# The last layer of a four-layer kernel scheduled anew: context part one batch ahead, product taken through the output weight first

## The chip, the cores and the metric

The kernel runs on one core of a Trainium2 chip. The metric is the device time of one execution, in microseconds; three runs of the kernel before gave 4614.44, 4619.2 and 4638.48 us, median 4619.2.

## The reference, cut to what matters

Four layers run one after the other on x (8 batches of 256 x 512, float32). The change touches only the last, a non-local block that takes the residual stream x and the context x_2, both per batch 256 channels by 512 positions:

```python
def _L3_xattn_ref(x, x_2, ...):
    B, C, CI, N = (16, 256, 128, 512); EPS = 1e-05
    g_x     = conv1x1(g_w, g_b, x_2).transpose(0, 2, 1)      # [b, 512, 128]
    theta_x = conv1x1(theta_w, theta_b, x).transpose(0, 2, 1)
    phi_x   = conv1x1(phi_w, phi_b, x_2)                     # [b, 128, 512]
    W = einsum('bnc,bcm->bnm', theta_x, phi_x) / 512
    y = einsum('bnm,bmc->bnc', W, g_x).transpose(0, 2, 1)
    wy = conv1x1(w_w, w_b, y)
    wy = bn_gamma * (wy - bn_mean) * rsqrt(bn_var + EPS) + bn_beta
    return wy + x
```

No softmax stands between the products, so they may be taken in any order. Both kernels first form M = phi g / 512 (128 x 128, from the context alone). The kernel before then has Y = M' theta and O = w_w Y.

## The kernel before, in words

The kernel is built by `layer0` to `layer3`, each with its own buffers, its own semaphores and one program per engine; a barrier ends each layer. Layer 2 ends with two stores of x3T to DRAM (L1783). Layer 3 works on 8 batches (B = 8), one after another, in rolled loops (`Fori`) on all engines. P = 128, E = 512, L = 256, CI = 128, LC = 2 (channel chunks), EC = 4 (position chunks). Everything in layer 3 is float32.

SyncE (SP) first adds 128 to each of its 21 semaphores (`start_ahead`, L2614, helper at L47), so that waits on a loop counter's value are never on zero; then it loads six constants (L2616) and, per batch, XT (the layer's input, transposed, L2623) and C (the context, L2624), once TensorE has finished with the batch before: there is one buffer of each.

TensorE per batch: eight 128x128 transposes of XT into banks 0 and 1 (L2643); eight matmuls for phi and g of the four position chunks, C the stationary operand, moving width 256, into banks 2 and 3 (L2649); two for theta, width 512 (L2654); four for M, width 128 (L2658); one for Y, width 512 (L2662); two for O, width 512, again into banks 2 and 3 (L2665). The profile counts each float32 matmul as two MATMUL instructions, except the transposes, which are one each.

ScalarE copies the transposed input out to X (L2678), theta with its bias to TH (L2680), and Y (L2682). VectorE adds the phi and g bias (L2698, writes PG), scales M (L2701), then per output chunk applies scale and shift of the batch norm (L2705), drains (L2706, which frees the banks for the next L2649), adds X (L2707) and drains (L2708, which frees X for the next L2678). GpSimd (POOL) stores the whole 256 x 512 output of a batch in one DMA from its queue (L2631), and lets O be written again when the store has landed.

The order around the change is thus set by the program order of each engine and by the semaphores; nothing is planned at run time.

Of the kernel before, what the change touches and what calls it, by code (L numbers as in the profile page):

```python
# [2577 lines left out]
def layer3(nc, x3T, ctx, theta_w, pg_w, pg_b, w_w, vec3, ident_in, out):  # L2578
    with ExitStack() as stack:
        def sb(name, shape, dt=F32):  # L2580
            return stack.enter_context(nc.sbuf_tensor("d_" + name, shape, dt))
# [24 lines left out]
        names = "consts_in memset_done bn_sqrt bn_in x_in in_used x_ps x_ready pg_ps pg_ready m_ps m_ready th_ps th_ready y_ps y_ready o_ps o_read out_ready out_free passed".split()  # L2606
        (consts_in, memset_done, bn_sqrt, bn_in, x_in, in_used, x_ps, x_ready, pg_ps, pg_ready, m_ps, m_ready, th_ps, th_ready,
         y_ps, y_ready, o_ps, o_read, out_ready, out_free, passed) = [sem(n) for n in names]
        out_stored = stack.enter_context(nc.semaphore("d_out_stored"))
        block = stack.enter_context(nc.Block())  # L2610

        @block.sync
        def _(sp):
            start_ahead(sp, sems)  # L2614
            for dst, src in ((WT[:, :, :], theta_w), (WPG[:, :, :], pg_w), (BPG[:, :], pg_b), (WW[:, :], w_w), (VEC[:, :], vec3), (ID[:, :], ident_in)):
                sp.dma_start(dst, src).then_inc(consts_in, 16)  # L2616
            with sp.Fori(0, B) as b:

                sp.wait_ge(x_ps, b + AHEAD)
                sp.sem_inc(passed, 1)  # L2620
                sp.wait_ge(pg_ps, b + AHEAD)
                sp.sem_inc(passed, 1)
                sp.dma_start(XT[:, :, :], x3T[b]).then_inc(x_in, 16)  # L2623
                sp.dma_start(C[:, :, :], ctx[b].rearrange("(k p) t -> p k t", p=P)).then_inc(x_in, 16)  # L2624
        @block.gpsimd
        def _(pool):
            pool.memset(EPS[:, :], LN_EPS).then_inc(memset_done, 1)
            with pool.Fori(0, B) as b:
                pool.wait_ge(out_ready, b + 1 + AHEAD)
                pool.sem_inc(passed, 1)  # L2630
                pool.dma_start(out[b].rearrange("(k p) t -> p k t", p=P), O[:, :, :]).then_inc(out_stored, 16)  # L2631
                pool.wait_ge(out_stored, (b + 1) * 16)
                pool.sem_inc(out_free, 1)

        @block.tensor
        def _(pe):
            pe.wait_ge(consts_in, 96 + AHEAD)
            pe.wait_ge(memset_done, 1 + AHEAD)
            with pe.Fori(0, B) as b:
                pe.wait_ge(x_in, (b + 1) * 32 + AHEAD)  # L2640
                for c in range(LC):
# [17 lines left out]
                mm.then_inc(m_ps, 1)
                pe.wait_ge(m_ready, b + 1 + AHEAD)  # L2660
                pe.wait_ge(th_ready, b + 1 + AHEAD)
                pe.matmul(ps[:, 6, :], M[:, :], TH[:, :], start=True, stop=True).then_inc(y_ps, 1)  # L2662
                pe.wait_ge(y_ready, b + 1 + AHEAD)
# [4 lines left out]
        @block.scalar
        def _(act):
            act.wait_ge(memset_done, 1 + AHEAD)  # L2670
            act.wait_ge(consts_in, 96 + AHEAD)
# [2 lines left out]
            with act.Fori(0, B) as b:
                act.wait_ge(x_ps, b + 1 + AHEAD)

                act.wait_ge(in_used, b + AHEAD)
                act.activation(X[:, :, :], ps[:, 0:2, :], ACT.Copy).then_inc(x_ready, 1)  # L2678
                act.wait_ge(th_ps, b + 1 + AHEAD)
                act.activation(TH[:, :], ps[:, 5, :], ACT.Identity, bias=VEC[:, V3_TB:V3_TB + 1]).then_inc(th_ready, 1)  # L2680
                act.wait_ge(y_ps, b + 1 + AHEAD)
                act.activation(Y[:, :], ps[:, 6, :], ACT.Copy).then_inc(y_ready, 1)  # L2682

        @block.vector
        def _(dve):
            dve.wait_ge(bn_sqrt, 1 + AHEAD)
# [9 lines left out]
            with dve.Fori(0, B) as b:  # L2696
                dve.wait_ge(pg_ps, b + 1 + AHEAD)
                dve.tensor_tensor(PG[:, :, :], ps[:, 2:4, :].rearrange("p a (c t) -> p (a c) t", c=2),  # L2698
                                  BPG[:, :].unsqueeze(1).broadcast_to([P, EC, 2 * CI]), ALU.add).then_inc(pg_ready, 1)
                dve.wait_ge(m_ps, b + 1 + AHEAD)  # L2700
                dve.tensor_scalar(M[:, :], ps[:, 4, 0:CI], 1.0 / E, None, ALU.mult).then_inc(m_ready, 1)  # L2701
                dve.wait_ge(o_ps, b + 1 + AHEAD)
                dve.wait_ge(out_free, b + AHEAD)
                for c in range(LC):
                    dve.tensor_scalar(O[:, c, :], ps[:, 2 + c, :], BN[:, 0, c:c + 1], BN[:, 1, c:c + 1], ALU.mult, ALU.add)  # L2705
                dve.drain().then_inc(o_read, 1)  # L2706
                dve.tensor_tensor(O[:, :, :], O[:, :, :], X[:, :, :], ALU.add).then_inc(out_ready, 1)  # L2707
                dve.drain().then_inc(in_used, 1)  # L2708
# [120 lines left out]
```

## Time and profile before

| quantity | value |
|---|---|
| median of 3 runs | 4619.2 us (4614.44 to 4638.48) |
| the profiled execution | 4615.37 us, span 4613.7 us |
| mean granted TensorE clock | 0.966 of full speed |
| TensorE matmul busy, whole kernel | 4238.2 us (92%) |
| VectorE busy | 2998.3 us (65%) |
| ScalarE busy | 1928.3 us (42%) |
| GpSimd busy | 1659.0 us (36%) |
| last matmul of layer 2 starts | 4487.84 us |
| first work of TensorE in layer 3 | 4505.61 us |
| end of the span | 4613.7 us |

Times are from the start of the span. The span runs from the first to the last instruction. A busy TensorE means that some matmul is in flight: matmuls are pipelined, and the distance between starts is what one costs. The granted clock is the share of full TensorE speed that the chip allowed in a stretch.

### The profile page before, as it was taken

What the parts mean: (1) busy time and instruction counts of PE and PEld (TensorE: products, weight loads), DVE (VectorE), ACT (ScalarE), POOL (GpSimd) and SP (SyncE); (2) the same over time, 40 slices, a digit from 0 to 9 for tenths busy, and PEclk for the clock granted to TensorE, in tenths of its full rate; (3) what the DMA queues carried; (4) which work ended last, traced back from release to release, by engine and by line L of the source; (5) the groups of instructions that cost most, each with busy time, mean ns of one, the idle gap of its engine ahead of it and who ended that gap; (6) DMA issues with size and microseconds to landing.
All of it is one profiled execution on the core that took longest, in us unless ns stands there. A gap on an engine that the chain in (4) does not pass through costs nothing. (4 is left out here: it accounts for less than half of the span.)

```text
span 4613.7 us, 72508 instructions
## 1 busy us (share of the span) xinstructions
PE 4238.2 (92%) x22864; PEld 3208.3 (70%) x22864; DVE 2998.3 (65%) x6494; ACT 1928.3 (42%) x3748; POOL 1659.0 (36%) x1139
## 2 busy tenths in 40 slices
PE   6999999578999997599999999999999999999987
PEld 3444444356777775488787797887887877978864
DVE  5666665178888885375775775766767757757543
ACT  2555555212232321255552454552554534545511
POOL 1222342345555553233334323234333344332330
PEclk8999999789999997799999999999999999999999
DMA  1000000200000000222112312222222122122223
GB/s 38 25 23 25 19 24 10 115 5 10 15 15 15 15 19 10 68 68 74 61 60 71 99 60 69 65 65 81 86 65 70 60 67 90 57 73 61 61 69 115
DMA packets 126449, 242.02 MB, mean 52 GB/s; under 512 B 16884, under 2 KB 38132, under 8 KB 124928
## 3 DMA queue, kind: packets, MB, share of 16 engines
q1 hardware_dynamic: 123904, 230.61, 15.9%
q0 software_dynamic: 2304, 8.39, 0.4%
q8 instruction: 127, 2.08, 0.2%
q14 instruction: 114, 0.93, 0.1%
HBM read 221.91 MB, written 16.78 MB: 52 GB/s over the span
## 5 line engine op out<-in xcount | busy, mean ns | idle before, releaser
L1885 POOL TENSOR_TENSOR c_wl<-c_wr,c_wh 128x512 fp32r<-128x512 f32 (+1 forms) x576 | 823.2, 1441 | 1672.2 <-ACT c_wh L2197 1465.9
L2291 ACT ACTIVATE c_pr<-c_ps,c_nms 128x257 f32<-128x257 f32 x512 | 244.5, 478 | 481.8 <-DVE c_nms L2485 479.3
L583 ACT ACTIVATE a_ex<-a_ps 128x1024 f32<-128x1024 f32 x256 | 261.4, 1024 | 260.4 <-PE a_ps L419 260.3
L1482 DVE TENSOR_TENSOR_SCAN b_sb<-b_wt,b_s,b_ps 128x256 f32<-128x256 f32 x512 | 362.1, 736 | 11.7 <-DVE b_ps L1468 1.4
L683 DVE TENSOR_REDUCE a_nm<-a_ps 128x2 f32<-128x1024 f32 x256 | 311.4, 1221 | 81.0 <-PE a_ps L396 80.8
L1434 POOL TENSOR_TENSOR b_sb<-b_sb,b_rt 128x1024 f32<-128x1024 f32 x128 | 278.2, 2180 | 207.5 <-ACT b_sb L1363 122.3
L1944 PE MATMUL c_ps<-c_hh,c_wh 128*128 128x512 f32 x768 | 318.2, 414 | 33.3 <-POOL c_hl L1891 33.1
L1944 PE MATMUL c_ps<-c_gh,c_wh 128*128 128x512 f32 x768 | 307.9, 401 | 23.5 <-DVE c_gl L2523 17.7
L2197 ACT ACTIVATE c_wh<-c_wr 128x512 fp32r<-128x512 f32 (+1 forms) x464 | 316.3, 688 | 8.6 <-PE c_ps L1946 7.4
L1944 PE MATMUL c_ps<-c_wh,c_cth 128*128 128x256 f32 x1024 | 304.7, 298 | 9.3 <-DVE c_ctl L2438 5.0
L1946 PE MATMUL c_ps<-c_hh,c_wl 128*128 128x512 f32 x768 | 309.9, 403 | 0.0
L1945 PE MATMUL c_ps<-c_hl,c_wh 128*128 128x512 f32 x768 | 309.6, 403 | 0.0
L1946 PE MATMUL c_ps<-c_gh,c_wl 128*128 128x512 f32 x768 | 303.2, 395 | 0.0
L1945 PE MATMUL c_ps<-c_gl,c_wh 128*128 128x512 f32 x768 | 302.9, 394 | 0.0
L1946 PE MATMUL c_ps<-c_wh,c_ctl 128*128 128x256 f32 x1024 | 290.6, 284 | 0.0
L1945 PE MATMUL c_ps<-c_wl,c_cth 128*128 128x256 f32 x1024 | 289.5, 283 | 0.0
L433 PE MATMUL a_ps<-a_ex,a_vf 128*64 128x512 f32 x1024 | 278.9, 623 | 8.9 <-ACT a_ex L583 7.9
L2483 DVE TENSOR_REDUCE c_nm<-c_ps 128x1 f32<-128x257 f32 x512 | 214.9, 420 | 69.1 <-PE c_ps L1946 68.4
L1040 PE MATMUL b_ps<-b_xf,b_w 128*128 128x256 f32 x1024 | 238.2, 386 | 13.0 <-DVEq L1533 9.1
L1040 PEld LDWEIGHTS b_ps<-b_xf,b_w 128*128 128x128 f32 x1024 | 194.0, 193 | 48.2 <-issue 17.9
L2523 DVE TENSOR_TENSOR c_gl<-c_g,c_gh 128x512 fp32r<-128x512 f32 x128 | 95.4, 752 | 201.6 <-ACT c_gh L2278 201.6
L2479 DVE TENSOR_SCALAR c_pr<-c_pr,c_rs 128x257 f32<-128x257 f32 x512 | 184.8, 361 | 40.3 <-issue 0.8
(309 smaller groups left out, 10762.7 us busy)
## 6 DMA issues: line engine op xcount, KB each, us to landing
c_wr<-in_downs SPq DMA_DIRECT2D x192, 256.0 KB, 2.7
c_wr<-in_wv SPq DMA_DIRECT2D x64, 512.0 KB, 3.8
c_wr<-in_wk SPq DMA_DIRECT2D x128, 256.0 KB, 2.9
c_wr<-in_wq SPq DMA_DIRECT2D x128, 256.0 KB, 2.7
c_wr<-in_fc SPq DMA_DIRECT2D x64, 256.0 KB, 2.8
b_w<-in_w SPq DMA_DIRECT2D x8, 1024.0 KB, 14.4
a_x<-in_x SPq DMA_DIRECT2D x8, 512.0 KB, 3.4
a_ctx<-in_ctx SPq DMA_DIRECT2D x8, 512.0 KB, 4.1
```

Of the source, the lines that this page charges most:

```text
L433: mm = pe.matmul(ps[64 * a:64 * a + VCOLS, BO, :], VF[:, k, g * HG + 2 * p + a, :], EX[:, n % 4, a, :], start=(k == 0), stop=(k == EC - 1) ...
L583: act.activation(EX[:, n % 4, :, :], ps[:, BT + 2 * (n % 2):BT + 2 * (n % 2) + 2, :], ACT.Exp).then_inc(ex_ready, 1)
L683: dve.tensor_reduce(NM[:, s, :].rearrange("p (h c) -> p h c", h=HG)[:, 2 * p:2 * p + 2, c:c + 1], ps[:, bank:bank + 2, :], AX.X, ALU.max, ...
L1040: mm = pe.matmul(half(bank, o), W[:, w, k, o * P:(o + 1) * P], src[:, k, :], start=(k == 0), stop=(k == EC - 1), skip_group_check=True)
L1434: pool.tensor_tensor(SB[:, quad % RING, :, 0:L], SB[:, quad % RING, :, 0:L], RT[:, third(b, q // 4), q // 4 % 2, :].unsqueeze(1).broadcast ...
L1482: mm = dve.tensor_tensor_scan(SB[:, quad % RING, r, 1:L + 1], WT[:, third(b, c), c % 2, :], half(spread_bank(pair), r), S0[:, b % 2, c, 4 ...
L1885: pool.tensor_tensor(piece(WL, slot), piece(WR, slot), piece(WH, slot), ALU.subtract).then_inc(piece_cut[slot], 1)
L1944: pe.matmul(out, sh, mh, start=start, stop=False, skip_group_check=True)
L1945: pe.matmul(out, sh, ml, start=False, stop=False, skip_group_check=True)
L1946: return pe.matmul(out, sl, mh, start=False, stop=stop, skip_group_check=True)
L2197: act.activation(piece(WH, slot), piece(WR, slot), ACT.Copy).then_inc(piece_high[slot], 1)
L2291: act.activation(PR[:, i, 0:L + 1], ps[:, BS + 1 - i % 2, 0:L + 1], ACT.Exp, bias=NMS[:, i:i + 1], scale=float(K2) ** -0.5, accum_out=RS[: ...
```

## The change: what it does

The input buffers XT and C, the output buffer O and a new buffer XB have two halves, used by batch parity. All five programs are unrolled in Python (no `Fori`), so no semaphore is moved ahead. TensorE does turn and phi_and_g (the first two steps) of batch b+1 before the last step of batch b. M is formed with its operands swapped, so that one matmul of width 256 can take it through the output weight: N = M' w_w (128 x 256); then O = N' theta, two matmuls of width 512, into banks 6 and 7. Y is gone. ScalarE also writes XB, which is X plus the shift of the batch norm, per chunk. VectorE ends a chunk with one scalar_tensor_tensor (O = scale * psum + XB) and no drain; each chunk is stored on its own from SP's queue. The constants are issued partly from SP, partly from ScalarE, in an order by need. The diff, without the lists of semaphore names and, from the SP program on, without most removed lines (they are printed above):

```diff
-        XT = sb("xt", [P, EC, L])
-        C = sb("c", [P, LC, E])
+        XT = sb("xt", [P, 2, EC, L])
+        C = sb("c", [P, 2, LC, E])
         X = sb("x", [P, LC, E])
+        XB = sb("xb", [P, 2, LC, E])
         PG = sb("pg", [P, EC, 2 * CI])
         M = sb("m", [P, CI])
+        N = sb("n", [P, L])
         TH = sb("th", [P, E])
-        Y = sb("y", [P, E])
-        O = sb("o", [P, LC, E])
+        O = sb("o", [P, 2, LC, E])
...
+        xt_in = [sem(f"xt_in{i}") for i in range(2)]
+        c_in = [sem(f"c_in{i}") for i in range(2)]
+        out_stored = [sem(f"out_stored{i}") for i in range(2)]
+        BXT, BPGS, BMN, BTH, BOUT = 0, 2, 4, 5, 6
...
 
         @block.sync
         def _(sp):
...
+            def load_ctx(b):
+                sp.dma_start(C[:, b % 2], ctx[b].rearrange("(k p) t -> p k t", p=P)).then_inc(c_in[b % 2], 16)
+            def load_x(b):
+                sp.dma_start(XT[:, b % 2], x3T[b]).then_inc(xt_in[b % 2], 16)
+            sp.dma_start(WPG[:, :, :], pg_w).then_inc(pg_in, 16)
+            load_ctx(0)
+            load_x(0)
+            sp.dma_start(WT[:, :, :], theta_w).then_inc(w_in, 16)
+            load_ctx(1)
+            load_x(1)
+            for b in range(B):
+                if b + 2 < B:
+                    sp.wait_ge(pg_ps, b + 1)
+                    load_ctx(b + 2)
+                    sp.wait_ge(x_ps, b + 1)
+                    load_x(b + 2)
+                for c in range(LC):
+                    sp.wait_ge(o_read, b * LC + c + 1)
+                    sp.dma_start(out[b, c * P:(c + 1) * P], O[:, b % 2, c, :]).then_inc(out_stored[b % 2], 16)
+            for i in range(2):
+                sp.wait_ge(out_stored[i], B // 2 * LC * 16)
         @block.gpsimd
         def _(pool):
             pool.memset(EPS[:, :], LN_EPS).then_inc(memset_done, 1)
...
 
         @block.tensor
         def _(pe):
...
+            def turn(b):
+                if b >= 1:
+                    pe.wait_ge(xb_ready, b)
+                if b == 0:
+                    pe.wait_ge(x_const_in, 3 * 16)
+                pe.wait_ge(xt_in[b % 2], (b // 2 + 1) * 16)
                 for c in range(LC):
                     for k in range(EC):
...
+                        mm = pe.transpose(ps[:, BXT + c, k * P:(k + 1) * P], XT[:, b % 2, k, c * P:(c + 1) * P], ID[:, :])
                 mm.then_inc(x_ps, 1)
 
...
+            def phi_and_g(b):
+                if b == 0:
+                    pe.wait_ge(pg_in, 16)
+                pe.wait_ge(c_in[b % 2], (b // 2 + 1) * 16)
                 for m in range(EC):
                     for k in range(LC):
...
+                        mm = pe.matmul(ps[:, BPGS + m // 2, (m % 2) * L:(m % 2 + 1) * L], C[:, b % 2, k, m * P:(m + 1) * P], WPG[:, k, :],
                                        start=(k == 0), stop=(k == LC - 1), skip_group_check=True)
                 mm.then_inc(pg_ps, 1)
...
+            def product(b):
+                pe.wait_ge(pg_ready, b + 1)
+                for m in range(EC):
+                    mm = pe.matmul(ps[:, BMN, 0:CI], PG[:, m, CI:], PG[:, m, 0:CI], start=(m == 0), stop=(m == EC - 1), skip_group_check=True)
+                mm.then_inc(m_ps, 1)
+            def theta(b):
+                if b == 0:
+                    pe.wait_ge(w_in, 2 * 16)
+                pe.wait_ge(x_ready, b + 1)
                 for k in range(LC):
...
+                    mm = pe.matmul(ps[:, BTH, :], WT[:, k, :], X[:, k, :], start=(k == 0), stop=(k == LC - 1))
                 mm.then_inc(th_ps, 1)
...
+            def through_w(b):
+                pe.wait_ge(m_ready, b + 1)
+                pe.matmul(ps[:, BMN, CI:CI + L], M[:, :], WW[:, :], start=True, stop=True, skip_group_check=True).then_inc(n_ps, 1)
+            def result(b):
+                pe.wait_ge(n_ready, b + 1)
+                pe.wait_ge(th_ready, b + 1)
                 for c in range(LC):
...
+                    if b >= 1:
+                        pe.wait_ge(o_read, (b - 1) * LC + c + 1)
+                    pe.matmul(ps[:, BOUT + c, :], N[:, c * P:(c + 1) * P], TH[:, :], start=True, stop=True).then_inc(o_ps, 1)
+            phi_and_g(0)
+            turn(0)
+            product(0)
+            theta(0)
+            through_w(0)
+            for b in range(B):
+                if b + 1 < B:
+                    turn(b + 1)
+                    phi_and_g(b + 1)
+                result(b)
+                if b + 1 < B:
+                    product(b + 1)
+                    theta(b + 1)
+                    through_w(b + 1)
 
         @block.scalar
         def _(act):
...
+            for dst, src in ((BPG[:, :], pg_b), (ID[:, :], ident_in), (VEC[:, :], vec3)):
+                act.dma_start(dst, src).then_inc(x_const_in, 16)
+            act.dma_start(WW[:, :], w_w).then_inc(w_in, 16)
+            act.wait_ge(memset_done, 1)
+            act.wait_ge(x_const_in, 3 * 16)
             act.activation(BN[:, 0, :], VEC[:, V3_VAR:V3_VAR + 2], ACT.Sqrt, bias=EPS[:, 0:1]).then_inc(bn_sqrt, 1)
...
+            for b in range(B):
+                act.wait_ge(x_ps, b + 1)
+                if b >= 1:
+                    act.wait_ge(th_ps, b)
+                act.activation(X[:, :, :], ps[:, BXT:BXT + 2, :], ACT.Copy).then_inc(x_ready, 1)
+                if b == 0:
+                    act.wait_ge(bn_ready, 1)
+                if b >= 2:
+                    act.wait_ge(o_read, (b - 1) * LC)
+                for c in range(LC):
+                    mm = act.activation(XB[:, b % 2, c, :], ps[:, BXT + c, :], ACT.Identity, bias=BN[:, 1, c:c + 1])
+                mm.then_inc(xb_ready, 1)
+                act.wait_ge(th_ps, b + 1)
+                act.activation(TH[:, :], ps[:, BTH, :], ACT.Identity, bias=VEC[:, V3_TB:V3_TB + 1]).then_inc(th_ready, 1)
+                act.wait_ge(n_ps, b + 1)
+                act.activation(N[:, :], ps[:, BMN, CI:CI + L], ACT.Copy).then_inc(n_ready, 1)
 
         @block.vector
         def _(dve):
...
+            def add_bias(b):
+                dve.wait_ge(pg_ps, b + 1)
+                if b == 0:
+                    dve.wait_ge(x_const_in, 3 * 16)
+                dve.tensor_tensor(PG[:, :, :], ps[:, BPGS:BPGS + 2, :].rearrange("p a (c t) -> p (a c) t", c=2),
+                                  BPG[:, :].unsqueeze(1).broadcast_to([P, EC, 2 * CI]), ALU.add).then_inc(pg_ready, 1)
+            def take_product(b):
+                dve.wait_ge(m_ps, b + 1)
+                dve.tensor_scalar(M[:, :], ps[:, BMN, 0:CI], 1.0 / E, None, ALU.mult).then_inc(m_ready, 1)
+            def finish(b):
+                dve.wait_ge(xb_ready, b + 1)
+                if b >= 2:
+                    dve.wait_ge(out_stored[b % 2], b // 2 * LC * 16)
+                for c in range(LC):
+                    dve.wait_ge(o_ps, b * LC + c + 1)
+                    dve.scalar_tensor_tensor(O[:, b % 2, c, :], ps[:, BOUT + c, :], BN[:, 0, c:c + 1], XB[:, b % 2, c, :], ALU.mult, ALU.add).then_inc(o_read, 1)
+            dve.wait_ge(bn_sqrt, 1)
             dve.reciprocal(BN[:, 0, :], BN[:, 0, :])
             dve.tensor_tensor(BN[:, 1, :], VEC[:, V3_WB:V3_WB + 2], VEC[:, V3_MEAN:V3_MEAN + 2], ALU.subtract)
             dve.drain()
@@ -2693,20 +2768,15 @@
             dve.tensor_tensor(BN[:, 1, :], BN[:, 1, :], BN[:, 0, :], ALU.mult)
             dve.drain()
             dve.tensor_tensor(BN[:, 1, :], BN[:, 1, :], VEC[:, V3_BETA:V3_BETA + 2], ALU.add)
...
+            dve.drain().then_inc(bn_ready, 1)
+            add_bias(0)
+            take_product(0)
+            for b in range(B):
+                if b + 1 < B:
+                    add_bias(b + 1)
+                finish(b)
+                if b + 1 < B:
+                    take_product(b + 1)
 
 
 def _l0(I):
```

## Rows read from the trace of the kernel before

**Rows 1.** The chain of waits, 4480 us to the end: shares by line.

```profile
by line: PE d_ps L2649 22.6%; PE d_ps L2665 11.4%; PE d_ps L2654 9.8%; PE d_ps L2662 6.5%; PE d_ps L2658 5.2%; DVE d_o L2705 4.6%; DVEq L2706 4.3%; ACT d_y L2682 3.5%; issue 3.4%; DMA d_c<-in_ctx 3.3%; SPq L2616 1.8%; DVE d_m L2701 1.7%; PE
```

**Rows 2.** Stretches: their us, busy us per engine, granted clock, DMA share, GB/s.

```profile
4440.00:4488.00 48.00, 48.00 (x208) 38.54 (x206) 22.54 (x35) 5.51 (x8) 18.10 (x14) 1.00 0.20 60
4488.00:4505.60 17.60, 0.22 (x1) 0.00 (x0) 1.72 (x7) 1.58 (x2) 0.10 (x1) 0.59 0.50 161
4533.90:4546.10 12.20, 10.31 (x42) 6.67 (x42) 4.27 (x5) 2.31 (x3) 0.73 (x1) 1.00 0.37 129
```

**Rows 3.** Timeline of one batch: start, us, engine, line, operation [idle before].

```profile
4533.91 3.72 PE L2649 MATMUL d_ps<-d_wpg,d_c 128*128 128x256 f32 x16 [0.87 <-DVEq L2706]
4533.95 1.22 DVE L2707 TENSOR_TENSOR d_o<-d_o,d_x 128x1024 f32<-128x1024 f32 x1
4535.26 1.02 ACT L2678 ACTIVATE d_x<-d_ps 128x1024 f32<-128x1024 f32 x1 [5.12 <-DVEq L2708]
4537.47 1.88 PE L2654 MATMUL d_ps<-d_x,d_wt 128*128 128x512 f32 x4
4537.67 1.23 DVE L2698 TENSOR_TENSOR d_pg<-d_ps,d_bpg 128x1024 f32<-128x1024 f32 x1 [2.50 <-PE d_ps L2649]
4538.95 1.10 PEld L2658 LDWEIGHTS d_ps<-d_pg 128*128 128x128 f32 x8 [0.43 <-DVE d_pg L2698]
4539.19 1.05 PE L2658 MATMUL d_ps<-d_pg 128*128 128x128 f32 x8
4539.39 0.69 ACT L2680 ACTIVATE d_th<-d_ps,d_vec 128x512 f32<-128x512 f32 x1 [3.11 <-PE d_ps L2654]
4540.62 1.12 PE L2662 MATMUL d_ps<-d_th,d_m 128*128 128x512 f32 x2 [0.38 <-DVE d_m L2701]
4541.79 0.60 ACT L2682 ACTIVATE d_y<-d_ps 128x512 f32<-128x512 f32 x1 [1.71 <-PE d_ps L2662]
4542.44 1.98 PE L2665 MATMUL d_ps<-d_y,d_ww 128*128 128x512 f32 x4 [0.69 <-ACT d_y L2682]
4544.26 1.04 PE L2643 MATMUL d_ps<-d_id,d_xt 128*128 128x128 f32 x8
4544.55 1.53 DVE L2705 TENSOR_SCALAR d_o<-d_ps,d_bn 128x512 f32<-128x512 f32 x2 [3.98 <-PE d_ps L2665]
4546.16 3.72 PE L2649 MATMUL d_ps<-d_wpg,d_c 128*128 128x256 f32 x16 [0.87 <-DVEq L2706]
```

**Rows 4.** The chain of waits into layer 3: start, us, what.

```profile
4495.59 0.02 SPq L47
...
4497.26 0.33 SPq L2616
...
4500.93 4.64 DMA d_c<-in_ctx
```

**Rows 5.** Stretches as in Rows 2: where the clock rises, and elsewhere.

```profile
4511.00:4512.00 1.00, 1.00 (x4) 0.80 (x4) 0.00 (x0) 0.00 (x0) 0.00 (x0) 0.65 0.00 0
...
1400.00:1500.00 100.00, 98.37 (x538) 77.76 (x537) 86.48 (x130) 29.97 (x63) 60.02 (x29) 1.00 0.02 6
...
4390.00:4400.00 10.00, 5.45 (x11) 3.38 (x12) 6.30 (x8) 2.52 (x4) 5.93 (x4) 0.50 0.15 39
```

**Rows 6.** Timeline of the last batch's end.

```profile
4607.45 1.23 DVE L2707 TENSOR_TENSOR d_o<-d_o,d_x 128x1024 f32<-128x1024 f32 x1
4609.42 0.72 POOL L2631 DMA_DIRECT2D out<-d_o  x1 [11.52 <-DVE d_o L2707]
```

**Rows 7.** Layer 2's operation of the added kind, by line: ns min/median/max.

```profile
L2386 DVE SCALAR_TENSOR_TENSOR c_x<-c_ps,c_vec,c_x x48: 733/750/753, 2184.9 to 4488.3; 128x512 f32<-128x512 f32 x48
```

**Rows 8.** DMA issues by line: KB each, median us from issue to landing.

```profile
d_c<-in_ctx SPq DMA_DIRECT2D x8, 512.0 KB, 4.8
out<-d_o POOLq DMA_DIRECT2D x8, 512.0 KB, 3.1
...
c_wr<-in_downs SPq DMA_DIRECT2D x192, 256.0 KB, 2.7
```

More of the change, by code:

```diff
@@ L2581, in sb @@
             return stack.enter_context(nc.sbuf_tensor("d_" + name, shape, dt))
-        sems = []
         def sem(name):
-            sems.append(stack.enter_context(nc.semaphore("d_" + name)))
-            return sems[-1]
+            return stack.enter_context(nc.semaphore("d_" + name))
         WT = sb("wt", [P, LC, CI])
@@ L2596, in layer3 @@
         BN = sb("bn", [P, 2, 2])
-        XT = sb("xt", [P, EC, L])
-        C = sb("c", [P, LC, E])
+        XT = sb("xt", [P, 2, EC, L])
+        C = sb("c", [P, 2, LC, E])
         X = sb("x", [P, LC, E])
+        XB = sb("xb", [P, 2, LC, E])
         PG = sb("pg", [P, EC, 2 * CI])
         M = sb("m", [P, CI])
+        N = sb("n", [P, L])
         TH = sb("th", [P, E])
-        Y = sb("y", [P, E])
-        O = sb("o", [P, LC, E])
+        O = sb("o", [P, 2, LC, E])
         ps = stack.enter_context(nc.psum_tensor("d_ps", [P, 8, 512], F32))
[L2606 to L2609, printed above, removed]
+        names = "pg_in x_const_in w_in memset_done bn_sqrt bn_ready x_ps x_ready xb_ready pg_ps pg_ready m_ps m_ready th_ps th_ready n_ps n_ready o_ps o_read".split()
+        (pg_in, x_const_in, w_in, memset_done, bn_sqrt, bn_ready, x_ps, x_ready, xb_ready, pg_ps, pg_ready, m_ps, m_ready, th_ps, th_ready,
+         n_ps, n_ready, o_ps, o_read) = [sem(n) for n in names]
+        xt_in = [sem(f"xt_in{i}") for i in range(2)]
+        c_in = [sem(f"c_in{i}") for i in range(2)]
+        out_stored = [sem(f"out_stored{i}") for i in range(2)]
+        BXT, BPGS, BMN, BTH, BOUT = 0, 2, 4, 5, 6
         block = stack.enter_context(nc.Block())
@@ L2613, in _ @@
         def _(sp):
[L2614 to L2624, printed above, removed]
+            def load_ctx(b):
[19 more added lines that the diff above has]
+                sp.wait_ge(out_stored[i], B // 2 * LC * 16)
         @block.gpsimd
@@ L2627, in _ @@
             pool.memset(EPS[:, :], LN_EPS).then_inc(memset_done, 1)
[L2628 to L2633, printed above, removed]
         @block.tensor
         def _(pe):
-            pe.wait_ge(consts_in, 96 + AHEAD)
@@ L2638, in _ @@
-            pe.wait_ge(memset_done, 1 + AHEAD)
-            with pe.Fori(0, B) as b:
-                pe.wait_ge(x_in, (b + 1) * 32 + AHEAD)
+            def turn(b):
[4 more added lines that the diff above has]
+                pe.wait_ge(xt_in[b % 2], (b // 2 + 1) * 16)
                 for c in range(LC):
                     for k in range(EC):
-                        mm = pe.transpose(ps[:, c, k * P:(k + 1) * P], XT[:, k, c * P:(c + 1) * P], ID[:, :])
+                        mm = pe.transpose(ps[:, BXT + c, k * P:(k + 1) * P], XT[:, b % 2, k, c * P:(c + 1) * P], ID[:, :])
@@ L2644, in _ @@
                 mm.then_inc(x_ps, 1)
-                pe.wait_ge(o_read, b + AHEAD)
+            def phi_and_g(b):
+                if b == 0:
+                    pe.wait_ge(pg_in, 16)
+                pe.wait_ge(c_in[b % 2], (b // 2 + 1) * 16)
                 for m in range(EC):
                     for k in range(LC):
-                        mm = pe.matmul(ps[:, 2 + m // 2, (m % 2) * L:(m % 2 + 1) * L], C[:, k, m * P:(m + 1) * P], WPG[:, k, :],
+                        mm = pe.matmul(ps[:, BPGS + m // 2, (m % 2) * L:(m % 2 + 1) * L], C[:, b % 2, k, m * P:(m + 1) * P], WPG[:, k, :],
@@ L2650, in _ @@
                                        start=(k == 0), stop=(k == LC - 1), skip_group_check=True)
                 mm.then_inc(pg_ps, 1)
-                pe.wait_ge(x_ready, b + 1 + AHEAD)
+            def product(b):
[7 more added lines that the diff above has]
+                pe.wait_ge(x_ready, b + 1)
@@ L2653, in _ @@
                 for k in range(LC):
-                    mm = pe.matmul(ps[:, 5, :], WT[:, k, :], X[:, k, :], start=(k == 0), stop=(k == LC - 1))
+                    mm = pe.matmul(ps[:, BTH, :], WT[:, k, :], X[:, k, :], start=(k == 0), stop=(k == LC - 1))
                 mm.then_inc(th_ps, 1)
-                pe.wait_ge(pg_ready, b + 1 + AHEAD)
-                for m in range(EC):
-                    mm = pe.matmul(ps[:, 4, 0:CI], PG[:, m, 0:CI], PG[:, m, CI:], start=(m == 0), stop=(m == EC - 1))
@@ L2659, in _ @@
[L2659 to L2663, printed above, removed]
-                for c in range(LC):
-                    mm = pe.matmul(ps[:, 2 + c, :], WW[:, c * P:(c + 1) * P], Y[:, :], start=True, stop=True)
-                mm.then_inc(o_ps, 1)
+            def through_w(b):
+                pe.wait_ge(m_ready, b + 1)
+                pe.matmul(ps[:, BMN, CI:CI + L], M[:, :], WW[:, :], start=True, stop=True, skip_group_check=True).then_inc(n_ps, 1)
@@ L2668, in _ @@
         @block.scalar
         def _(act):
-            act.wait_ge(memset_done, 1 + AHEAD)
-            act.wait_ge(consts_in, 96 + AHEAD)
-            act.activation(BN[:, 0, :], VEC[:, V3_VAR:V3_VAR + 2], ACT.Sqrt, bias=EPS[:, 0:1]).then_inc(bn_sqrt, 1)
[L2674 to L2682, printed above, removed]
+            for dst, src in ((BPG[:, :], pg_b), (ID[:, :], ident_in), (VEC[:, :], vec3)):
+                act.dma_start(dst, src).then_inc(x_const_in, 16)
@@ L2684, in _ @@
         @block.vector
         def _(dve):
-            dve.wait_ge(bn_sqrt, 1 + AHEAD)
+            def add_bias(b):
[7 more added lines that the diff above has]
+                dve.tensor_scalar(M[:, :], ps[:, BMN, 0:CI], 1.0 / E, None, ALU.mult).then_inc(m_ready, 1)
@@ L2695, in _ @@
             dve.tensor_tensor(BN[:, 1, :], BN[:, 1, :], VEC[:, V3_BETA:V3_BETA + 2], ALU.add)
[L2696 to L2708, printed above, removed]
+            dve.drain().then_inc(bn_ready, 1)
[7 more added lines that the diff above has]
+                    take_product(b + 1)
 def _l0(I):
```

## The prediction

> **What bounds the kernel now.** The change touches one stage, so I read that stage and not the whole. The chain of waits over the last 134 us [rows 1] belongs by two thirds to TensorE's lines of layer 3; no transfer has over 3.4%. The table of stretches [rows 2] says the same more carefully: while layer 2 still runs, TensorE is busy 48.00 of 48.00 us; then it does next to nothing from 4488 to 4505.6; and in a batch of layer 3 it is busy 10.31 of 12.2 us, VectorE 4.27, ScalarE 2.31, DMA share 0.37. Nothing is full, so the batch is a loop of handovers. The timeline of one batch [rows 3] shows them. The reader should follow TensorE's starts, not its busy time. One batch is 4546.16 - 4533.91 = 12.25 us.
>
> What TensorE itself needs comes from the same rows. Where one group follows another without a wait, the distance of starts is the price: L2649 4537.47 - 4533.91 = 3.56 us for 16 instructions of width 256; L2654 4539.19 - 4537.47 = 1.72 us for four of width 512. L2649 and L2654 are in flight for 3.72 and 1.88, so the tail behind the last start adds 0.16; taking it off, L2658 costs 1.05 - 0.16 = 0.89 and L2643 1.04 - 0.16 = 0.88. The sum before: 0.88 + 3.56 + 1.72 + 0.89 + 0.96 (L2662, 1.12 - 0.16, or 0.86 as half of L2654) + 1.72 = 9.6 to 9.7 us. So about 2.6 us of the 12.25 are no work: the way from M over L2662, ScalarE's 0.60 us copy of Y and L2665, and the wait of L2649 for VectorE's two L2705 operations and their drain (0.87 us in the row, after the transposes had filled part of it).
>
> **The change, part by part.**
>
> *The batch.* TensorE now needs turn 0.88, phi_and_g 3.56, result 1.72 (the shape of L2665, priced as L2654), product 0.89, theta 1.72, and through_w, two instructions of width 256: 2/16 of 3.56 = 0.44. Together 9.21 us; Y's 0.86 is traded for 0.44. Does anything still wait? I go through the pass from its start S. ScalarE: the last N copy has to end before X; X can start when the transposes are out, S + 1.1, takes 1.02, then XB twice, 0.69 each by L2680 (two new operations per batch, hidden), done at S + 3.5; turn of the next pass needs it at S + 9.2. TH and N come at the end of the pass; result needs N only after the next turn and phi_and_g, 4.4 us later. VectorE: add_bias starts 0.20 us after phi_and_g stops issuing (4537.47 to 4537.67) and takes 1.23, and product needs it after result's 1.72. Rows 3 have exactly this pair, with L2654 in result's place: the weight load waits until 4538.95, but the matmul starts at 4539.19, where the one before lets it. So the margin is just about nil, and it does hold. Then two scalar_tensor_tensor at 0.75 [rows 7], ending near S + 7.4, in place of 1.53 plus drain plus 1.22, and the scaling of M, ready near S + 7.8, while through_w asks at S + 8.8. SP: the loads of b+2 stand in its queue behind the two stores of b-1, issued near S + 8.5 of pass b-1; turn(b+2) starts at S + 18.4 of the same clock. That leaves 9.9 us for transfers that land in 4.8 us [rows 8]. The bytes per batch are unchanged (1.57 MB), 170 instead of 129 GB/s. Bounds for the pass: 9.21 (no handover costs anything) and 12.25 less the 0.42 of work traded away and the 0.87 of the drain wait, 10.96 (all other waits come back elsewhere). I take 9.25, next to the lower bound, since each wait was placed. The last seven passes with a following batch then take 64.75 us.
>
> *The start.* SP's chain [rows 4] begins at 4495.59 with the semaphore increments of L47 and comes to its first load at 4497.26; then come six constants, and C is issued at 4500.93, landing 4.64 us later; TensorE starts at 4505.61. Without the increments WPG goes out near 4495.6, C near 4496.1, XT near 4496.5 (issues are 0.4 to 0.5 apart). With the same 4.64 us, phi_and_g(0) can start at 4500.7. Bounds: 4498.8 (the 2.7 us of a 256 KB load) and 4502.4 (4.64 plus the 1.7 us by which SP's head start could be something else than increments). The XT half and ScalarE's four small loads ride beside it; they are needed 6 us later.
> The Trainium skill (DMA: Bandwidth & Descriptors, Issuing engines are not separate DMA queues) says that transfers started from several engines share the same DMA engines and save issue time only. It speaks against the part that moved constants to ScalarE: by it they slow C a little. No row here prices that.
>
> TensorE starts cold, now as before. Before, the granted clock was 0.50 from 4505.6 and rose inside the slice 4511 to 4512, whose mean is 0.65 [rows 5], so near 4511.7: 6.1 us at 1.2 GHz after 17 idle us, costing 3.05. I take the same after 12.5 idle us; between 4 and 8 us cold is plus or minus 1. Then: phi_and_g(0) issues 3.05 of its 3.56 us of work in 6.1 us, so it ends at 4507.3; turn(0) ends at 4508.2; add_bias(0) at 4507.3 + 0.20 + 1.23 = 4508.7, product starts 0.24 later at 4508.95 (one real gap, 0.75 us); X is copied by 4508.2 + 0.2 + 1.02 = 4509.4, before product ends at 4509.85; theta(0) to 4511.55, through_w(0) to 4512.0. The batch norm's constants need ScalarE's table load and are done by about 4503.
>
> *The end.* 4512.0 + 64.75 = 4576.75, where through_w(7) stops issuing. ScalarE: theta ended 0.44 earlier, so TH runs 4576.5 to 4577.2; N, half as wide as the 0.60 us copy of Y, I take as 0.45 (0.3 to 0.6): 4577.65. Two result matmuls, 1.98 with the tail: 4579.7. One scalar_tensor_tensor: 4580.5. The store's issue 0.2 later, landing in 3.0 (the POOL store of twice the size took 3.1, a 256 KB load 2.7) [rows 8]: 4583.7. From the landing to the end of the span were 4613.7 - 4609.42 - 3.1 = 1.2 us [rows 6]: 4584.9. The old end also had L2706's and L2707's work and 0.7 us between VectorE's end and POOL's issue.
> The skill's page on DMA (Anatomy of one DMA) gives a fixed 2.0 us plus size over 436 GB/s: an estimate of 3.2 us for the old 512 KB store, which the row bears out with 3.1, and 2.6 for the new one; the end would come 0.4 us earlier.
>
> *Sum.* 4613.7 - 4584.9 = 28.8 us: 4.9 from the earlier start, 3.0 in each of seven passes (21.0), and 2.9 over the first pass and the end. The profiled execution took 4615.4 us, 3.8 below the median of the runs; 28.8 off the median gives 4590 us. Layers 0 to 2 have the same code.
>
> **Rivals.** *The handover to product opens.* The margin above is nil, so any delay of add_bias goes into every pass one for one, as do weight loads that wait for semaphores. With 0.5 to 1.2 us a pass the time is 4594 to 4598, mid 4596. For: the 0.43 us wait of the weight load in rows 3. Against: its matmul lost nothing. Chance 0.12.
>
> *The loads come late.* If a batch's two loads took over 9.9 us, or SP were held up by a store, TensorE would wait at every turn. At a period of 10.7 us it is 7 x 1.45 = 10 us more: 4600. Against: 4.8 us landing, DMA share 0.37. Chance 0.03.
>
> *The change doesn't do what it says at the edge:* SP's first load waits for something other than the increments, or the cold stretch grows; 3 to 4 us are lost, 4594. Chance 0.08.
>
> *The clock falls (slower).* TensorE would be busy without a pause in float32, and if the chip then granted only 1.2 GHz, a pass would take 18.4 us: seven passes cost 64 us more, 4654 us. It decides once a pass is over 12.25 + 7.8/7 = 13.4 us. Against: 0.50 stands where TensorE was half idle (5.45 of 10 us busy), 1.00 where it was busy 98.37 of 100 us with about as many instructions, in straight-line code of layer 1, and 48 of 48 us [rows 2, 5]. Straight-line fetching would show there too: layer 1 runs 10.7 loads and matmuls per us, the new pass 9. Chance 0.02.
>
> **How the numbers follow.** The forecast, 4590 us, has 0.75. Its own range, 4584 to 4595, is the spread of the runs' median against the profiled one (3.8), the start (+1.7, -1.9) and the cold stretch (1). The range to 4600 takes in the handover and the edge. A measurement of this kernel tells about 0.5% from no change, 23.1 us, which lies at 4596.1. The forecast and the edge rival are faster but for the tail of the noise, half of the handover rival too: faster 0.84; same 0.13, from the handover, late loads and runs with a high median; slower 0.03, the clock and what I don't see.
>
> **What would show it.** Right: TensorE's first matmul of the layer near 4501; starts of phi_and_g 9.2 to 9.3 us apart with clock 1.00; DMA share near 0.5; L2705's successor at 0.75 us each; the span's end 8 us after the last through_w. Handover: an idle time before product's matmuls on VectorE's add. Late loads: TensorE's transposes waiting for a DMA. Wrong altogether: a period near 11 or more, or a clock below 1.00 after the first 7 us of the layer.

## The result

Five runs of each: 4581.44 us (4578.03 to 4590.57) after, 4623.08 us (4614.44 to 4638.48) before; ratio 0.9916, interval 0.9896 to 0.9936. A second measurement (experiment 8) gave 4583.34 against 4617.25 us, ratio 0.9927, interval 0.9908 to 0.9945. The change makes the kernel faster by 34 to 42 us; I had forecast 29. Both medians lie below the forecast's own range of 4584 to 4595 us, by 2.6 and 0.7 us.

The profiled execution took 4585.26 us, span 4583.6. To compare spans I count from the start of layer 2's last matmul, since the time that layers 0 to 2 take varies from one execution to the next: that start fell at 4487.84 us before and at 4491.55 after, and between 4486.30 and 4498.45 us over the eight profiles whose layers 0 to 2 have the same code. From there to the end of the span, called L below, it is 125.9 us before and 92.1 after.

The stretches of the profile after, columns as in [rows 2], over 50 us of the layer:

```profile
4520.00:4570.00 50.00, 50.00 (x237) 36.71 (x236) 15.45 (x23) 17.17 (x28) 0.00 (x0) 1.00 0.48 169
```

TensorE never stops, its clock is full, VectorE and ScalarE are a third busy. One pass in the timeline of the profile after (the weight loads but for one, SP's issues and ScalarE's TH and N are left out):

```profile
4523.01 1.04 PE L2656 MATMUL d_ps<-d_id,d_xt 128*128 128x128 f32 x8
...
4523.88 3.62 PE L2666 MATMUL d_ps<-d_wpg,d_c 128*128 128x256 f32 x16
4524.08 1.02 ACT L2725 ACTIVATE d_x<-d_ps 128x1024 f32<-128x1024 f32 x1 [0.34 <-PE d_ps L2656]
4525.00 1.26 ACT L2731 ACTIVATE d_xb<-d_ps,d_bn 128x512 f32<-128x512 f32 x2
...
4527.34 1.88 PE L2696 MATMUL d_ps<-d_th,d_n 128*128 128x512 f32 x4
4527.54 1.22 DVE L2746 TENSOR_TENSOR d_pg<-d_ps,d_bpg 128x1024 f32<-128x1024 f32 x1 [6.19 <-PE d_ps L2666]
...
4528.68 1.40 DVE L2760 SCALAR_TENSOR_TENSOR d_o<-d_ps,d_bn,d_xb 128x512 f32<-128x512 f32 x2
4528.81 1.10 PEld L2674 LDWEIGHTS d_ps<-d_pg 128*128 128x128 f32 x8 [0.43 <-DVE d_pg L2746]
4529.05 1.05 PE L2674 MATMUL d_ps<-d_pg 128*128 128x128 f32 x8
...
4529.94 1.88 PE L2682 MATMUL d_ps<-d_x,d_wt 128*128 128x512 f32 x4
4530.14 0.29 DVE L2751 TENSOR_SCALAR d_m<-d_ps 128x128 f32<-128x128 f32 x1
...
4531.66 0.59 PE L2688 MATMUL d_ps<-d_ww,d_m 128*128 128x256 f32 x2
...
4532.09 1.04 PE L2656 MATMUL d_ps<-d_id,d_xt 128*128 128x128 f32 x8
```

Start to start it is 4532.09 - 4523.01 = 9.08 us (9.09 over the seven passes), against 12.25 in [rows 3]. No PE row has an idle time. L2760, the scalar_tensor_tensor of the two chunks, stands where L2705 and L2707 were; it ends at 4530.08, just before M's scaling begins.

The beginning and the end, from the timeline after, with C's transfer from the chain of waits:

```profile
4499.27 0.33 SPq L2622 DMA_DIRECT2D d_wpg<-in_pg_w  x1
...
4499.65 0.43 SPq L2617 DMA_DIRECT2D d_c<-in_ctx  x1
4499.65 4.34 DMA d_c<-in_ctx
...
4504.13 5.33 PE L2666 MATMUL d_ps<-d_wpg,d_c 128*128 128x256 f32 x16 [12.19 <-DMA d_c<-in_ctx]
4506.28 1.28 ACT L2720 ACT_TABLE_LOAD   x1 [19.09 <-DMA d_vec<-in_vec]
...
4513.49 0.59 PE L2688 MATMUL d_ps<-d_ww,d_m 128*128 128x256 f32 x2
...
4578.31 1.98 PE L2696 MATMUL d_ps<-d_th,d_n 128*128 128x512 f32 x4 [0.62 <-ACT d_n L2736]
...
4579.58 1.51 DVE L2760 SCALAR_TENSOR_TENSOR d_o<-d_ps,d_bn,d_xb 128x512 f32<-128x512 f32 x2 [3.70 <-PE d_ps L2696]
```

TensorE's granted clock (the number before the DMA share) is 0.50, which is 1.2 GHz, in the first of these half-microsecond stretches, and rises in the second:

```profile
4506.63:4507.13 0.50, 0.50 (x2) 0.41 (x2) 0.00 (x0) 0.50 (x1) 0.00 (x0) 0.50 1.07 418
4507.13:4507.63 0.50, 0.50 (x3) 0.38 (x3) 0.00 (x0) 0.49 (x2) 0.00 (x0) 0.68 1.07 434
```

### The profile page after: what moved, and what is told of

It reads as the page before. It is cut to its first block and busy times, and to the rows that moved or that the text cites. A ratio compares the mean times of both kernels' runs of the same rounds, so it can differ in the third digit from the quotient of the medians.

```text
span 4583.6 us, 72278 instructions
## 1 busy us (share of the span) xinstructions
PE 4231.7 (92%) x22864; PEld 3209.4 (70%) x22864; DVE 2987.3 (65%) x6486; ACT 1935.0 (42%) x3764; POOL 1652.9 (36%) x1131
```

## The experiments

Kernels 1 to 7 were run once each, with the profile; experiments 8 and 9 time the changed kernel and kernel 7 over several runs. "Cold" is the time from TensorE's first matmul in layer 3 to where its clock rises from 1.2 GHz, from half-microsecond stretches. All columns are in us.

| kernel | TensorE starts after layer 2's last matmul | cold | a pass | L |
|---|---|---|---|---|
| before | 17.8 | 6.1 | 12.25 | 125.9 |
| 5 unrolled | 16.6 | 2.8 | 12.16 | 121.8 |
| 2 Y again | 12.7 | 3.2 | 10.62 | 104.4 |
| 1 at once | 12.6 | 4.5 | 10.48 | 102.3 |
| 4 old finish | 12.8 | 4.2 | 9.29 | 95.9 |
| 3 delay | 12.6 | 2.9 | 9.29 | 93.7 |
| after | 12.6 | 3.3 | 9.09 | 92.1 |
| after, experiment 8 | 13.1 | 4.1 | 9.09 | 93.0 |
| 6 preload | 7.8 | 5.8 | 9.09 | 88.6 |
| 7 early work | - | - | 9.09 | 84.2 |

### 5: the kernel before, written out

```diff
-            start_ahead(sp, sems)
...
-            with pe.Fori(0, B) as b:
-                pe.wait_ge(x_in, (b + 1) * 32 + AHEAD)
+            for b in range(B):
+                pe.wait_ge(x_in, (b + 1) * 32)
```

> The kernel before with layer 3's loops written out and, with them, no semaphore moved ahead and no passed counter; nothing else. Yardstick L, from the start of layer 2's last matmul to the end of the span: before 125.9 us (4613.7 - 4487.84), after 92.1 (4583.6 - 4491.55). My theory: the increments are 1.67 us of the start and the turn of the loop about 0.1 us a batch, so TensorE starts 16.1 us after layer 2's last matmul instead of 17.8, a batch takes 12.15 and L is 123.4. Rival (rolled loops cost TensorE or the waits much more, and a good part of the gain is the unrolling): a batch of 11.7 or less, L under 121.

```profile
4496.75 0.33 SPq L2615 DMA_DIRECT2D d_wt<-in_theta_w  x1
...
4499.97 5.55 DMA d_c<-in_ctx
...
4518.15 1.04 PE L2641 MATMUL d_ps<-d_id,d_xt 128*128 128x128 f32 x8
...
4530.31 1.04 PE L2641 MATMUL d_ps<-d_id,d_xt 128*128 128x128 f32 x8
```

Measured: L 121.8 for the 123.4 expected, a batch 12.16 us. That is 0.09 us a batch, as forecast. The increments were worth what I had read from [rows 4]: SP's first load went out 7.7 us after layer 2's last matmul (4489.04 here) in place of 9.4. But TensorE started only 1.2 us earlier and not 1.7, since C, issued 2.2 us earlier, took 5.55 us for 4.64. The cold stretch was 3.3 us shorter, which alone is 1.6 of the 4.1 us. Unrolling is not where the time went.

### 1: the result at once, nothing between N and its use

```diff
             for b in range(B):
+                result(b)
                 if b + 1 < B:
                     turn(b + 1)
                     phi_and_g(b + 1)
-                result(b)
-                if b + 1 < B:
+                    theta(b + 1)
                     product(b + 1)
-                    theta(b + 1)
                     through_w(b + 1)
...
```

> The changed kernel, but the context part of the next batch is not put between N and its use: result(b) stands right behind through_w(b), and theta in front of product as in the kernel before; VectorE finishes the batch first. My theory: each handover that loses its cover comes back at its own price: N's copy 0.78 us (4578.31 - 4577.10 less the 0.43 of issue, in the changed kernel's last batch) and M's scaling about 0.5, so a pass is 9.09 + 1.28 = 10.4 us and L 101. Rival (the interleaving matters little, the gain is the shorter chain of operations): 9.1 to 9.5 us, L 92 to 95.

Its timeline:

```profile
4517.89 1.05 PE L2674 MATMUL d_ps<-d_pg 128*128 128x128 f32 x8
...
4519.33 0.70 PE L2688 MATMUL d_ps<-d_ww,d_m 128*128 128x256 f32 x2 [0.38 <-DVE d_m L2750]
4520.06 0.38 ACT L2735 ACTIVATE d_n<-d_ps 128x256 f32<-128x256 f32 x1 [1.28 <-PE d_ps L2688]
4520.50 1.98 PE L2696 MATMUL d_ps<-d_th,d_n 128*128 128x512 f32 x4 [0.47 <-ACT d_n L2735]
```

A pass is 10.48 us for the 10.4 expected. From product's start to the next step's it is 1.44 instead of the changed kernel's 0.89, from through_w's 1.17 instead of 0.43, and from result's 1.82 instead of 1.72: 1.39 us together. My theory holds: each handover returns at its own price, 0.55 for M and 0.74 for N.

### 2: Y again

```diff
...
-                pe.matmul(ps[:, BMN, CI:CI + L], M[:, :], WW[:, :], start=True, stop=True, skip_group_check=True).then_inc(n_ps, 1)
+                pe.wait_ge(th_ready, b + 1)
+                pe.matmul(ps[:, BTH, :], M[:, :], TH[:, :], start=True, stop=True).then_inc(n_ps, 1)
...
-                    pe.matmul(ps[:, BOUT + c, :], N[:, c * P:(c + 1) * P], TH[:, :], start=True, stop=True).then_inc(o_ps, 1)
+                    pe.matmul(ps[:, BOUT + c, :], WW[:, c * P:(c + 1) * P], N[:, :], start=True, stop=True).then_inc(o_ps, 1)
...
-                act.activation(N[:, :], ps[:, BMN, CI:CI + L], ACT.Copy).then_inc(n_ready, 1)
+                act.activation(N[:, :], ps[:, BTH, :], ACT.Copy).then_inc(n_ready, 1)
```

> The changed kernel, but with Y again: M with its operands as before, Y = M' TH (width 512) in through_w's place, its copy 128x512, and O = w_w Y. Everything else, the batch ahead too, stays. My theory: Y costs 0.43 us more matmul than N, and it needs TH, which comes 0.95 us after theta stops issuing, where N needed M alone; a pass is 9.09 + 1.38 = 10.5 us, L about 103. Rival (only the shorter matmul counts): 9.5 us, L about 95.5.

```profile
4519.89 1.88 PE L2682 MATMUL d_ps<-d_x,d_wt 128*128 128x512 f32 x4
4520.09 0.29 DVE L2752 TENSOR_SCALAR d_m<-d_ps 128x128 f32<-128x128 f32 x1
4521.81 0.69 ACT L2735 ACTIVATE d_th<-d_ps,d_vec 128x512 f32<-128x512 f32 x1 [5.60 <-PE d_ps L2682]
4522.64 1.10 PE L2689 MATMUL d_ps<-d_th,d_m 128*128 128x512 f32 x2 [0.87 <-ACT d_th L2735]
```

M was there at 4520.38, but Y needs TH, which ends at 4522.50. Theta to Y is 2.75 us where theta to N was 1.72 (+1.03), and Y to the transposes 0.93 for 0.43 (+0.50): 10.62 us. In this order of steps, the gain of taking M through the weight first is two thirds independence from theta, one third arithmetic. Y with theta ahead of product I did not run: there it would wait for M, as through_w does in experiment 1, which cost 0.55, so an estimate of the first part against that order is 0.55 and not 1.03.

### 4: VectorE's old finish

```diff
...
-                    dve.scalar_tensor_tensor(O[:, b % 2, c, :], ps[:, BOUT + c, :], BN[:, 0, c:c + 1], XB[:, b % 2, c, :], ALU.mult, ALU.add).then_inc(o_read, 1)
+                    dve.tensor_scalar(O[:, b % 2, c, :], ps[:, BOUT + c, :], BN[:, 0, c:c + 1], BN[:, 1, c:c + 1], ALU.mult, ALU.add)
+                dve.drain()
+                dve.tensor_tensor(O[:, b % 2, :, :], O[:, b % 2, :, :], XB[:, b % 2, :, :], ALU.add).then_inc(o_read, LC)
```

> The changed kernel, but VectorE ends a batch as before: two tensor_scalar, a drain, one add of 128x1024; XB is then a plain copy, and both chunks are stored after the add. My theory: M's scaling comes behind the longer finish and reaches through_w 0.3 us late, so a pass is about 9.4 us; the end grows by 1.3; L 95.4. Rival (VectorE has slack, busy 15.45 of 50 us): a pass of 9.09, L 93.4.

```profile
4519.39 1.23 DVE L2762 TENSOR_TENSOR d_o<-d_o,d_xb 128x1024 f32<-128x1024 f32 x1
4520.53 0.28 DVE L2751 TENSOR_SCALAR d_m<-d_ps 128x128 f32<-128x128 f32 x1
4520.87 0.30 PEld L2688 LDWEIGHTS d_ps<-d_ww,d_m 128*128 128x128 f32 x2 [0.76 <-DVE d_m L2751]
```

M comes late, as the theory said: the weight load waits for it, and a pass is 9.29 us, 0.20 longer where I had 0.3. So the single operation is worth 1.4 us over seven passes to TensorE, though VectorE, busy 18.28 of 40 us here, has slack on average.

### 3: a delay in front of the bias add

```diff
...
+                dve.tensor_tensor(SPARE[:, :], WPG[:, 0, :], WPG[:, 1, :], ALU.add)
                 dve.tensor_tensor(PG[:, :, :], ps[:, BPGS:BPGS + 2, :].rearrange("p a (c t) -> p (a c) t", c=2),
```

> The changed kernel with one more VectorE operation (128x256, two SBUF operands, about 0.33 us) between the end of phi_and_g and the bias add. My theory: add_bias reaches product with no margin (its end at 4519.67, the weight load at 4519.73, the matmul at 4519.97 in line), so the delay goes into every pass, 9.09 + 0.3 = 9.4 us, L (from the start of layer 2's last matmul to the end) 92.1 + 2.5 = 94.6. Rival (TensorE has some slack there, since the weight load could start later): a pass of 9.09 to 9.2, L 92 to 93.

```profile
4526.82 1.88 PE L2697 MATMUL d_ps<-d_th,d_n 128*128 128x512 f32 x4
4527.03 0.43 DVE L2747 TENSOR_TENSOR d_spare<-d_wpg 128x256 f32<-128x256 f32 x1 [6.19 <-PE d_ps L2667]
...
4527.37 1.22 DVE L2748 TENSOR_TENSOR d_pg<-d_ps,d_bpg 128x1024 f32<-128x1024 f32 x1
...
4528.64 0.97 PEld L2675 LDWEIGHTS d_ps<-d_pg 128*128 128x128 f32 x8 [0.77 <-DVE d_pg L2748]
4528.64 1.16 PE L2675 MATMUL d_ps<-d_pg 128*128 128x128 f32 x8
```

The add came 0.34 us later (4527.37 - 4527.03), a pass grew by 0.20 to 9.29. So the margin was 0.14 us, small but not nil. It has two parts: the late weight load and its matmul start together, at 4528.64, while the one in time went 0.24 ahead (4528.81 and 4529.05 in the pass shown for the changed kernel), which takes up 0.24 of the delay; and the eight matmuls behind the late load were in flight 1.16 us instead of 1.05, which gives 0.1 back. The direction was mine, the size between the two.

### 8: the changed kernel again

> The changed kernel once more, timed against the kernel before in five rounds. In the profiles its last stretch (from layer 2's last matmul to the end) is 33.8 us shorter, of which some 1.4 us is a shorter cold stretch that may fall either way; the medians of the runs stood 41.6 us apart. My theory: the change acts in layer 3 alone, the rest is scatter of layers 0 to 2; the medians are 32 to 34 us apart, ratio 0.993. Rival (layers 0 to 2 run faster as well): 40 us or more, ratio 0.991 or less.

Medians 33.9 us apart, six runs against eleven, ratio 0.9927 (0.9908 to 0.9945). My theory expected 32 to 34. L was shorter by 33.8 in the first two profiles and by 32.9 with the profile of this experiment (125.9 - 93.0); the 41.6 of the first measurement needs no gain in layers 0 to 2.

### 6, 7 and 9: what still stood before TensorE

In the changed kernel TensorE waits some 12 us between the layers. Half of layer 2's x buffer and its context buffer are dead in its last pair of batches. Kernel 6 loads into them; kernel 7 also works ahead of the barrier:

```diff
...
+            sp.wait_ge(out_stored, (NPAIR - 1) * 32)
+            sp.wait_ge(ct_ready, NPAIR + AHEAD)
+            for dst, src in ((D["WPG"], pg_w), (D["C"], ctx[0].rearrange("(k p) t -> p k t", p=P)), (D["XT"], x3T[0]),
+                             (D["BPG"], pg_b), (D["ID"], ident_in), (D["VEC"], vec3), (D["WT"], theta_w), (D["WW"], w_w)):
+                sp.dma_start(dst, src).then_inc(D["early_in"], 16)
             store(NPAIR - 1)
...
+            pe.wait_ge(early["early_in"], 128)
+            for m in range(EC):
+                for k in range(LC):
+                    pe.matmul(ps[:, 2 + m // 2, (m % 2) * L:(m % 2 + 1) * L], early["C"][:, k, m * P:(m + 1) * P], early["WPG"][:, k, :],
+                              start=(k == 0), stop=(k == LC - 1), skip_group_check=True)
...
```

The second part, at the end of layer 2's TensorE program, is in kernel 7 alone; the transposes of batch 0 follow it.

> The changed kernel, but the constants, context 0 and x3T[0] of layer 3 are loaded during layer 2, into dead halves of two of its buffers, from SP's queue ahead of the last store. My theory: TensorE's start waits for nothing but the barrier and the load of context 0; with it loaded, it starts 7.8 us after layer 2's last matmul instead of 12.6, and L is 92.1 - 4.8 = 87.3 (give or take 1.5 for the cold stretch, 3.4 to 6.1 us so far). Rival (another wait takes its place: the loads of batch 1, issued only then, or ScalarE's table): L 89 to 92.

> As the preloading kernel, and phi_and_g(0) and turn(0) run on TensorE behind layer 2's last matmul, ahead of the barrier; VectorE adds bias 0 before it makes the batch norm's constants, ScalarE copies X before the square root. My theory: the 6.5 us of these two steps leave the way, part of them comes back since the clock may fall in the wait for the barrier; through_w(0) stops issuing 12.2 to 15.2 us after layer 2's last matmul instead of 22.4, L is 82 to 85. Rival: TensorE's later arrival at the barrier, or batch 1's loads, cost as much as it saves: L 87 or more.

The timeline of 6, then of 7:

```profile
4489.15 0.39 PE L1962 MATMUL c_ps<-c_gh,c_wl 128*128 128x512 f32 x1
...
4496.93 3.32 PE L2676 MATMUL d_ps<-c_ct,c_x 128*128 128x256 f32 x7 [7.38 <-PEq L1635]
```

```profile
4488.81 3.62 PE L2196 MATMUL c_ps<-c_ct,c_x 128*128 128x256 f32 x16
4492.27 1.04 PE L2200 MATMUL c_ps<-c_ct,c_x 128*128 128x128 f32 x8
...
4497.89 2.07 PE L2694 MATMUL c_ps<-d_pg 128*128 128x128 f32 x8 [4.59 <-DVE d_pg L2760]
```

In 6 TensorE starts 7.8 us after layer 2's last matmul, released by the barrier (PEq L1635), 4.8 us earlier, as forecast; the stretch at 1.2 GHz took 5.8 us this time, which is why L is 88.6 and not 87.3. In 7 through_w(0) stops issuing at 14.5 us (4503.11 - 4488.58), L is 84.2, both as forecast. Its granted clock, in two stretches after turn(0) ended at 4493.31 and in one when product and theta of batch 0 ran:

```profile
4494.58:4495.08 0.50, 0.00 (x0) 0.00 (x0) 0.00 (x0) 0.00 (x0) 0.00 (x0) 1.00 0.00 0
4495.58:4496.08 0.50, 0.00 (x0) 0.00 (x0) 0.00 (x0) 0.00 (x0) 0.00 (x0) 0.50 0.00 0
4500.00:4502.00 2.00, 2.00 (x3) 0.77 (x3) 0.36 (x2) 1.27 (x2) 0.00 (x0) 0.50 0.98 342
```

It was down to 1.2 GHz by 4495.58 and back up only in theta's last microsecond. Product took 1.86 us (4497.89 to 4499.75) instead of 0.89 and theta 2.93 (to 4502.68) instead of 1.72: 2.2 us of what moving the work ahead saved came back here.

> The kernel with layer 3's first loads, its first context part and its first transposes ahead of the barrier, timed. Its last stretch was 84.2 us against 92.1 of the changed kernel. My theory: 41 us below the kernel before, 8 below the changed kernel, ratio about 0.991. Rival (the early loads delay layer 2's last weight loads, or the barrier gives it back): no more than 4 us below the changed kernel.

Kernel 7 timed (experiment 9): 4574.81 us (4570.39 to 4577.38), 42 us below the kernel before, ratio 0.9903 (0.9883 to 0.9922), and 8.5 us below the changed kernel's 4583.34 in the same measurement; its slowest run is below the changed kernel's fastest, 4578.03. It beats both, as forecast.

## Why the prediction was right, and where it was off

The steps, all from layer 2's last matmul (4487.84 before, 4491.55 after):

| step | forecast | measured |
|---|---|---|
| phi_and_g(0) starts | 12.9 | 12.6 |
| from there to the end of through_w(0) | 11.3 | 9.8 |
| seven passes | 64.8 | 63.6 |
| from there to the end | 8.1 | 6.1 |
| L | 97.1 | 92.1 |

- **The batch.** Right in mechanism and nearly in size: 9.09 for 9.25 us. Of the 0.16, 0.10 is phi_and_g: 3.46 us from start to start where it follows the transposes directly (4523.88 to 4527.34), while the 3.56 of [rows 3] contained the slower start behind a wait. I had also added 0.04 for nothing. Experiments 5, 1 and 2 show what carries it: the unrolling 0.09; without the interleaving the pass is 1.39 longer, with Y 1.53 longer. Both of these kernels have O in banks of its own and the new finish, so the wait of L2649 for the drain, 0.87 us in [rows 3], is gone in each; I did not run that alone. With it the three come to 3.79, more than the 3.07 that remain, so they overlap: what each is worth by itself is shown only against the changed kernel.
- **The handover to product** did hold; its margin was 0.14 us and not nil, so a delay does not go into every pass one for one: 0.34 us of it cost 0.20 (experiment 3).
- **VectorE's finish** was argued to be hidden. It is: M is done at 4530.43, 0.8 us before through_w's weight load in line. The old finish would have been 0.20 too late in each pass (experiment 4).
- **The start.** Right: 12.6 for 12.9. SP's first load went out 7.7 us after layer 2's last matmul for the 7.8 I had, and C landed in 4.34 us instead of 4.64 with ScalarE's four loads beside it; no run leaves these out, so what they cost C is not shown. That it is the load that TensorE waits for is shown by experiment 6. The constants on ScalarE's queue came later than I thought: VEC, the third, landed after 5.8 us and the table load began at 4506.28, so the batch norm's shift was ready only near 4508.9, 17.3 us after layer 2's last matmul, where I had 15.2. Nothing waited, since XB needs it only at 4511.29.
- **The cold stretch** is one of two terms of the sum that were mis-sized, next to the end: 3.3 us against the 6.1 I carried over, worth 1.4. Over nine profiles it was 2.8 to 6.1 us with no order by kernel, by the idle time before, or by chip (2.9 and 5.8 on one and the same). The 6.1 of the kernel before was the longest of them, and one row cannot show that.
- **The end** was 2.0 us shorter, the largest miss. From VectorE's last result to the end I had 0.2 + 3.0 + 1.2 = 4.4 us, and it was 4583.6 - 4581.1 = 2.5. The stores of 256 KB landed in 2.0 us (median), for which I took 3.0. The Trainium skill (DMA: Bandwidth & Descriptors, Anatomy of one DMA) has its fit for transfers on GpSimd's path alone, so the 2.6 us worked out from it for a store on SP's queue is an estimate outside its case; it was nearer than 3.0 and still too long. That leaves 0.5 for the issue and all that follows the landing, where I had 0.2 and 1.2. The 1.2 that I had read from [rows 6] as a fixed tail is thus none: in the two kernels with POOL's store it is 1.2 and 1.0 (experiment 5), in those with SP's stores about 0.5. What in POOL's store makes the difference stays open.
- **The rivals.** Clock: 1.00 over 50 us of unbroken float32 matmuls. Late loads: DMA share 0.48, no TensorE wait for a DMA after the first. All as forecast.
- **The misses together.** The misses of the sum, 2.0 in the end, 1.4 in the cold stretch, 1.2 in the passes and 0.3 in the start, all have one sign, so L came out 5.0 us shorter than forecast, and none made up for another. The cold stretch could have come out long again; that it was short was luck.
- **The medians.** I added the profile's difference to a median of three runs. The scatter of layers 0 to 2 (12 us in where they end) is larger than every term I argued about but the seven passes; the second measurement, 33.9, agrees with the traces.

The landings that the end and the start rest on, by line of the profile after:

```profile
d_c<-in_ctx SPq DMA_DIRECT2D x8, 512.0 KB, 4.1
...
out<-d_o SPq DMA_DIRECT2D x16, 256.0 KB, 2.0
...
d_vec<-in_vec ACTq DMA_DIRECT2D x1, 5.5 KB, 5.8
```

## What to carry to other kernels

Price a serial stage by the distances between TensorE's starts where nothing waits; the rest of the period is what interleaving the next batch can win, and here all of it was won. When products may be reordered, choose the order in which the chain's middle does not need the other branch: here, with theta as the last step before it, two thirds of what N gained over Y came from not waiting for theta. And an engine that is busy less than half of the time can still be late at one handover (experiment 4): look at its order of operations there, not at its share.

## What the runs showed that I had not expected

- A transfer of 5.5 KB took 5.8 us to land, as the third of four on ScalarE's queue, with 1.3 MB issued on SP's queue just ahead of it; the 128 KB one first in its own queue took 3.2 us. The Trainium skill (DMA: Bandwidth & Descriptors, Issuing engines are not separate DMA queues) says that transfers started from different engines run on the same DMA engines and interleave. The trace agrees: the DMA share was 0.97 from the issue of the 5.5 KB to their landing.
- The time that TensorE stays at 1.2 GHz after an idle stretch varied from 2.8 to 6.1 us between executions, 1.6 us of run time between the extremes.
- How long the clock stays up behind the last matmul varied as well. In kernel 7 it fell about 2.0 us after the end of turn(0), and 2.3 in the profile of experiment 9; behind layer 2's last matmul it took about 3.0 us in the profile before and 5.3 in the profile after (the stretches below, in this order). TensorE's wait of 4.6 us in kernel 7 is shorter than that 5.3, so whether its 2.2 us always come back is not shown.

```profile
4491.00:4492.00 1.00, 0.00 (x0) 0.00 (x0) 0.00 (x0) 0.00 (x0) 0.00 (x0) 0.61 1.03 336
```

```profile
4497.00:4498.00 1.00, 0.00 (x0) 0.00 (x0) 0.00 (x0) 0.00 (x0) 0.00 (x0) 0.61 0.11 35
```
